# Attention and a block-quantized FFN on one core: ScalarE's jobs at the unit's end, VectorE's behind the value product

## The reference

```python
xn = layernorm(x)                                   # 4 x 1024 x 128
q, k, v = (split_heads(xn @ W + b) for W, b in ...) # 16 heads, 8 wide
scores = einsum('bhqd,bhkd->bhqk', q, k) * 8 ** -0.5 + slope[h] * (key_pos - query_pos)
attn = softmax(scores) @ v @ Wo + bo
def fp4(t):                                         # blocks of 16 along the last axis
    s = max(max(abs(t_block)) / 6, 1e-12)
    return grid[searchsorted(mid, abs(t / s))] * sign(t) * s
h = silu(fp4(xn) @ fp4(w_gate).T) * (fp4(xn) @ fp4(w_up).T)   # 352 wide
out = x + attn + fp4(h) @ fp4(w_down).T
```

## Time and profile before

| what | us |
|---|---|
| median of 3 runs | 901.35 |
| the profiled execution | 894.07 |
| its span (first to last instruction) | 892.3 |
| TensorE matmul busy | 772.9 |
| VectorE busy | 741.1 |
| ScalarE busy | 633.0 |
| GpSimd busy | 349.3 |
| mean granted TensorE clock | 0.962 |

### The profile page before, as it was taken

The page is one execution under the profiler, slowest core; times in us unless marked ns, Lnnn a source line. Parts: engine busy times, 40 slices in busy tenths (PEclk is TensorE's granted clock), DMA queues, the critical chain, the costliest instruction groups (busy, mean ns, idle before and its releaser), DMA issues.

```text
span 892.3 us, 13552 instructions
## 1 busy us (share of the span) xinstructions
PE 772.9 (87%) x4939; PEld 225.7 (25%) x4939; DVE 741.1 (83%) x878; ACT 633.0 (71%) x1262; POOL 349.3 (39%) x271
## 2 busy tenths in 40 slices
PE   3279989898989989897989989898989898979896
PEld 2012223221223323231323323222213231313222
DVE  7898898889888888978898888989897989898920
ACT  4106878777777878776877778777777687767775
POOL 7272172624226373715053553615152505141320
PEclk9557999999999999999999999999999999999999
DMA  5900020131001020320102020310102000000000
GB/s 156 256 13 2 1 72 3 52 92 36 3 13 37 13 72 2 101 44 1 37 2 49 13 73 1 107 37 1 37 2 49 13 3 1 2 1 2 2 1 24
DMA packets 32826, 31.83 MB, mean 36 GB/s; under 512 B 4344, under 2 KB 26552, under 8 KB 32760
## 3 DMA queue, kind: packets, MB, share of 16 engines
q1 hardware_dynamic: 32760, 30.96, 12.8%
HBM read 15.91 MB, written 15.04 MB: 35 GB/s over the span
## 4 chain that ended last, share of the span: by engine, by line
PE 58%; DVE 27%; ACT 8%; issue 4%; POOL 2%; DMA 1%; SPq 0%; ACTq 0%; DVEq 0%; POOLq 0%
PE low L966 22%; DVE neg_max L811 19%; PE mx L936 18%; ACT probs L630 6%; PE low L955 5%; PE mx L1005 3%; PE mx L989 3%; PE low L983 2%; DVE am L784 1%; DVE mb L804 1%; PE low L922 1%; ACT pv_s L667 1%; PE low L997 1%; DVE hid L826 1%; DVE inv L798 1%
## 5 line engine op out<-in xcount | busy, mean ns | idle before, releaser
L811 DVE TENSOR_REDUCE neg_max<-mx 128x1 f32<-128x1024 f32 x512 | 611.6, 1221 | 91.6 <-PE mx L936 80.2
L630 ACT ACTIVATE probs<-low 128x512 f32<-128x512 f32 x1024 | 552.0, 603 | 182.1 <-PE low L955 180.4
L936 PE MATMUL mx<-k_op,q_op 51*128 51x512 bf16 x1024 | 318.5, 398 | 55.9 <-DVE neg_max L811 33.4
L955 PE MATMUL low<-q_op,k_op 53*128 53x512 bf16 x1024 | 329.0, 389 | 8.0 <-ACT probs L630 2.5
L966 PE MATMUL low<-probs,v_op 128*32 128x512 f32 x2048 | 277.4, 614 | 7.1 <-ACT pv_s L667 5.9
L551 POOL TENSOR_SCALAR tanh_s<-tanh_s 128x704 f32<-128x704 f32 x16 | 31.7, 1982 | 313.7 <-ACT gate_s L681 313.7
L936 PEld LDWEIGHTS mx<-k_op,q_op 51*128 51x128 bf16 x1024 | 62.6, 95 | 358.5 <-DVE neg_max L811 197.2
L955 PEld LDWEIGHTS low<-q_op,k_op 53*128 53x128 bf16 x1024 | 68.5, 94 | 76.5 <-ACT probs L630 63.8
L489 POOL TENSOR_SCALAR mb<-mb 128x960 f32<-128x960 f32 (+2 forms) x17 | 58.8, 3456 | 39.6 <-DVE mb L804 37.9
L966 PEld LDWEIGHTS low<-probs,v_op 128*32 128x32 f32 x2048 | 40.5, 108 | 89.9 <-issue 46.1
L477 POOL TENSOR_TENSOR zb<-hid,inv 128x704 f32<-128x704 f32 x16 | 22.2, 1387 | 97.7 <-DVEq L799 97.7
(11 more groups left out here) (120 smaller groups left out, 522.3 us busy)
## 6 DMA issues: line engine op xcount, KB each, us to landing
q_op<-q_rows SPq DMA_DIRECT2D x32, 192.0 KB, 3.8
k_op<-k_rows SPq DMA_DIRECT2D x32, 192.0 KB, 4.7
q_rows<-qp SPq DMA_DIRECT2D x8, 384.0 KB, 2.6
k_rows<-kp SPq DMA_DIRECT2D x8, 384.0 KB, 3.2
x_s<-in_L_attn_inputs_dram SPq DMA_DIRECT2D x8, 256.0 KB, 3.7
q_rows<-qp SPq DMA_DIRECT2D x8, 256.0 KB, 3.1
k_rows<-kp SPq DMA_DIRECT2D x8, 256.0 KB, 3.1
out_dram<-o_s SPq DMA_DIRECT2D x8, 256.0 KB, 2.3
```

The lines of the kernel that those rows point to most:

```text
L630: nc.scalar.activation(probs[U % 3][:, 2 * g + x, :], bank("exp", U, j), ACT.Exp).then_inc(st_free, 1)
L811: nc.vector.tensor_reduce(to, slot("max", pos)[:], AX.X, ALU.max, negate=True).then_inc(mx_free, 1)
L936: ins = nc.tensor.matmul(slot("max", pos)[:, 512 * kh:512 * kh + 512], q, k, start=True, stop=True)
L955: nc.tensor.matmul(bank("exp", U, j), k_op[quad][r, g, kt * P:(kt + 1) * P], q_op[quad][r, g, half * HALF:(half + 1) * HALF], start=True, ...
```

## The change

- The unit's jobs are split in two. Jobs of ScalarE's ring (`end`) are done by TensorE behind the unit's value product and by ScalarE behind the unit's four exponentials. Jobs of VectorE's ring (`middle`) stay between the first and the second two pairs, and where a unit has one, the value product moves in front of it. In a unit without such a job the value product stays behind the last pair.
- ScalarE's copy pv_s comes behind the first exponential instead of the second.
- The lead is 23 chunks instead of 22, so one more chunk is reduced ahead of the loop and the last chunk of a half is a unit's i = 0 instead of i = 1 of the same unit. `HEAD` follows from the lead's parity, so that a chunk and the score beside it still use opposite row halves. The turn jobs stay in the same units.
- In a period up moves one unit later (5 instead of 4), the block maxima behind the second chunk of that unit, scales and inverses to unit 6, powers to unit 8, and GpSimd's steps with them. The projections start at unit 9 of a period instead of 3: xnT, q, k at 9, 10, 11 and v at 3 of the next; the splits of q and k follow both behind each other. SyncE's issues of parts and gathers hang on `group_unit` and move six units later.
- The inverses become a function of their own (`block_inverses`), behind the second chunk.

```diff
-LEAD = 22
+LEAD = 23
...
 def group_unit(g):
-    return 13 + 60 * (g // 2 - 1) + 15 * (g % 2)
+    return 19 + 60 * (g // 2 - 1) + 15 * (g % 2)
...
-HEAD = ((1, 0), (1, 1), (0, 0), (0, 1))
+HEAD = tuple((x, g) for x in ((LEAD + 1) % 2, LEAD % 2) for g in range(2))
...
     if 0 <= p < NP:
-        out += {0: [("xT", p)], 1: [("gate", p, 0)], 2: [("gate", p, 1)], 4: [("up", p)], 12: [("hT", p, 0)],
+        out += {0: [("xT", p)], 1: [("gate", p, 0)], 2: [("gate", p, 1)], 5: [("up", p)], 12: [("hT", p, 0)],
                 13: [("hT", p, 1)], 14: [("down", p)]}.get(f, [])
     for g in range(2, NG):
-        if 0 <= U - group_unit(g) < 4:
-            out.append((("xnT", "q", "k", "v")[U - group_unit(g)], g))
+        out += {0: [("xnT", g)], 1: [("q", g)], 2: [("k", g)], 9: [("v", g)]}.get(U - group_unit(g), [])
...
+def middle(U):
+
+    return [job for job in extras(U) if job[0] in IN_DVE_RING]
+
+
+def end(U):
+
+    return [job for job in extras(U) if job[0] not in IN_DVE_RING]
...
(rings)
-            for job in extras(U) if i == 0 else ():
-                (to_dve if job[0] in IN_DVE_RING else to_act)(*job)
+            for job in middle(U) if i == 0 else ():
+                to_dve(*job)
+        for job in end(U):
+            to_act(*job)
...
(GpSimd)
-                    if U == group_unit(g) + 2:
+                    if U == group_unit(g) + 4:
                         three_parts(g, 0, "q")
-                    if U == group_unit(g) + 3:
+                    if U == group_unit(g) + 4:
                         three_parts(g, 1, "k")
...
-                    if U == ffn_unit(p) + 5:
+                    if U == ffn_unit(p) + 6:
                         scale_to_grid(p + 1)
-                    if U == ffn_unit(p) + 7:
+                    if U == ffn_unit(p) + 8:
                         round_on_grid(p + 1)
...
(ScalarE)
-                for j in range(2):
+                for j in range(4):
                     exponential(U, j)
-                if U % KT == 1 and U > KT:
-                    m = U // KT - 1
-                    act.wait_ge(pv_done, U - 1)
-                    if m:
-                        act.wait_ge(mx_full, MX["pvT", m - 1] + 1)
-                    nc.scalar.copy(pv_s[:], pv).then_inc(pv_kept, 1)
-                for job in extras(U):
+                    if j == 0 and U % KT == 1 and U > KT:
+                        m = U // KT - 1
+                        act.wait_ge(pv_done, U - 1)
+                        if m:
+                            act.wait_ge(mx_full, MX["pvT", m - 1] + 1)
+                        nc.scalar.copy(pv_s[:], pv).then_inc(pv_kept, 1)
+                for job in end(U):
...
-                for j in range(2, 4):
-                    exponential(U, j)
...
(VectorE)
-                link(nc.vector.reciprocal(inv[:, 0:n], scn[:, 0:n]))
-                dve.sem_inc(inv_ok, 1)
+
+            def block_inverses(job):
+                n = job_cols(job) // BLK
+                settle()
+                nc.vector.reciprocal(inv[:, 0:n], scn[:, 0:n]).then_inc(inv_ok, 1)
...
-                    if i == 1:
-                        for job in extras(U):
-                            job_on_vector(job)
+                    for job in middle(U) if i == 1 else ():
+                        job_on_vector(job)
                     if pos < CHUNKS:
                         reduce_chunk(pos)
                     for p in range(NP):
-                        if U == ffn_unit(p) + 5 and i == 0:
+                        if U == ffn_unit(p) + 5 and i == 1:
                             block_maxima(p + 1)
-                        if U == ffn_unit(p) + 5 and i == 1:
-                            block_scales(p + 1)
-                        if U == ffn_unit(p) + 7 and i == 0:
+                        if U == ffn_unit(p) + 6:
+                            (block_scales if i == 0 else block_inverses)(p + 1)
+                        if U == ffn_unit(p) + 8 and i == 0:
                             powers(p + 1)
...
(TensorE)
-                    for job in extras(U) if i == 0 else ():
+                    if 0 < U <= NU and i == (0 if middle(U) else 1):
+                        value_product(U - 1)
+                    for job in middle(U) if i == 0 else ():
                         job_on_array(job)
-                if 0 < U <= NU:
-                    value_product(U - 1)
+                for job in end(U):
+                    job_on_array(job)
```

More of the change, by code:

```diff
@@ L795, in block_scales @@
                 mark(nc.vector.tensor_scalar(sc[:, 0:n], am[:, 0:n], 1.0 / 6.0, 1e-12, ALU.mult, ALU.max))
-                link(nc.vector.tensor_scalar(scn[:, 0:n], am[:, 0:n], (1.0 + 2.0 ** -22) / 6.0, 1e-12,
+                mark(nc.vector.tensor_scalar(scn[:, 0:n], am[:, 0:n], (1.0 + 2.0 ** -22) / 6.0, 1e-12,
                                              ALU.mult, ALU.max))
-                link(nc.vector.reciprocal(inv[:, 0:n], scn[:, 0:n]))
-                dve.sem_inc(inv_ok, 1)
+            def block_inverses(job):
+                n = job_cols(job) // BLK
+                settle()
+                nc.vector.reciprocal(inv[:, 0:n], scn[:, 0:n]).then_inc(inv_ok, 1)
             def powers(job):
@@ L872, in _ @@
             block_scales(0)
+            block_inverses(0)
             for pos in range(LEAD):
```

## The result

| | before | after |
|---|---|---|
| median of the runs, us | 900.57 (898.9 to 916.8, 4 runs) | 922.95 (919.77 to 924.45, 4 runs) |
| the profiled execution, us | 894.07 | 919.77 |
| its span | 892.3 | 918.0 |
| main loop, first score of unit 0 to first score of unit 255 | 66.67 to 880.36: 813.7 | 68.08 to 906.07: 838.0 |
| VectorE busy | 741.1 | 723.5 |

The ratio is 1.0255, 95% interval 1.0222 to 1.0288: slower by 22.4 us in the medians. The ratio leaves out executions that lie more than 1.5% above the fastest of their kernel, such as the one of 916.8 us. Of the 25.7 us between the two spans, 24.3 are in the main loop and 1.4 ahead of it, where one more chunk is reduced.

What follows compares the result with a forecast made beforehand. A loop of score, exponential, score, value product was taken to set 2.46 us per unit without a job. Terms summed to +20 us on 894.1 profiled, so 914; the runs' median lies 7.3 higher, so 921, range 898 to 942.

Steps and rivals of the forecast that it cites:

- gates at the end: 32 gate products behind the value product: each costs 1.08 us instead of 0.49, +18.9 us in all.
- projections at the end: xnT, q, k, v of six groups at the unit's end and in other units: +3.0 a group, +18 us.
- turn: 31 turn transposes at the unit's end: -7.4 us for place, -5 for TensorE's wait for neg_parts going, -12.4 together.
- product ahead of pvT, wo, bvo: Value product ahead of pvT fills TensorE's hole: -0.32 us for two units, some 20 times, -6.4 us.
- product ahead of up: In 16 units up's data come 1.0 us later; VectorE's holes leave 0.3 of it: +5 us.
- product ahead of down: In 16 units with down, 0.4 us each, estimated from up: +6.4 us.
- pv_s copy: ScalarE's copy behind the first exponential: value product 0.49 us earlier, except in 10 of 31 halves: -10.3 us.
- stretches at half clock: Shorter TensorE waits avoid an estimated three stretches at 1.2 GHz, 1 us each: -3 us.
- hT: 32 jobs of three transposes, about 0.5 us each at the unit's end, cost what a job costs now: 0.
- The first (slack covers the end jobs): Rival: VectorE or other slack covers gates and projections at the unit's end: 884 us on the runs' scale; chance 0.11.
- the second: Rival: maxima reach the scores late, each half waits 1 us: +31, 952 us; chance 0.07.
- the third: Rival: ten more stretches at half clock, 1.5 us each: +15, 936 us; chance 0.1.

Runs made afterwards that it cites:

- experiment 1: Kernel after with only the gate products back in the middle of their units: 906.32 us, ratio 1.0064.
- 2: Kernel after with xnT, q, k and v back in the middle, at the kernel after's units: 910.09 us, ratio 1.0105.
- 10: Kernel after with only the turn jobs back in the middle, lead 23 kept: 926.13 us, ratio 1.0275.
- 3: Kernel after with the value product last in every unit: 909.96 us, ratio 1.0099.
- experiment 9: Kernel after with the value product last again only in units with up: 906.86 us, ratio 1.0073.
- 5: Kernel after with the pv_s copy back behind the second exponential: 934.29 us, ratio 1.0383.
- experiment 11: Kernel before with only the pv_s copy moved behind the first exponential: 905.44 us, ratio 1.0084.
- 7: Kernel after with lead 22 instead of 23: 920.94 us, ratio 1.0236.
- 4: Kernel after with all of ScalarE's jobs in the middle, value product first only where all jobs are VectorE's: 918.66 us, ratio 1.0199.
- 6: Kernel after with only the hT transposes back in the middle: 934.15 us, ratio 1.0414.
- the mixture: Kernel after with gates, xnT, q, k, v, ctxT in the middle, value product first only for pvT, wo, bvo: 877.02 us, ratio 0.9785.

## Why the prediction was right, and where it was not

The time, the sign and the range came out (921 predicted, 922.95 measured), and most unit lengths that it named are in the trace: gates 3.25 and 3.57, pvT 2.87 and 2.71, pv_s 2.62, k 3.7 to 3.9, VectorE idle 1.2 ahead of `hid`. That the time came within 2 us is in part luck: the sum gave 914 us for the profiled execution, which took 919.77, and the 7.3 us that were added for the median of the runs are 3.2 in the kernel after. Term by term up was taken 9 us too low and turn's saving too high, and gates and projections were taken a little too high. The measured columns are what undoing a part in the kernel after gave, once by the medians against before and once by the unit lengths in the traces with the units at half clock left out:

| term | predicted | by the medians | by the units | run |
|---|---|---|---|---|
| gates at the end | +18.9 | +16.6 | +16.2 | 1 |
| projections at the end | +18 with the move | +12.9, the place alone | +10.0, and about +5 for the move | 2 |
| turn | -12.4 | -6.1, the place alone | -3.4 to -5, the place alone | 10 |
| product ahead of pvT, wo, bvo | -6.4 | -6.8 | -7.2 | 3 and 9 |
| product ahead of up | +5 | +13.2 | +13.8 | 9 |
| product ahead of down | +6.4 | | +6.6 | 3 |
| pv_s copy | -10.3 | -9.4 | -11.1 | 5 |
| stretches at half clock | -3 | | about -4 | before and after |
| one more chunk ahead of the loop | +1.2 | | +1.4 | span |

By the units the terms sum to +24 to +26 without the last line; the loops differ by 24.3. The medians differ by 22.4. The column by the medians has an error of some us in each line. Each part was undone with all others in place, so a sum need not be exact, and experiment 11 shows how far a term can depend on its surroundings.

- **Gates.** Right in mechanism and size: +0.30 and +0.62 in the two units, the rest in the successor. The 2 to 3 us that are missing are not worked out; some of the units behind a pair are paced by VectorE anyway.
- **Projections.** Right: 4.4 - 1.4 = 3.0 a group was predicted, and 4.2 - 1.4 = 2.8 is what the one group that can be compared shows. The runs undo the place only, 1.7 to 2.2 a group; the rest is the move.
- **Turn.** The place was taken at 7.4 us and gives some 5. The step "lead 23 puts the last chunk of a half at the start of a unit ..., so TensorE's wait of 19.4 us for neg_parts goes" came true in the wait, but experiments 7 and 10 show that the wait stays away without lead 23 and all but stays away without the end place. What took it away, and what its going is worth (the prediction counted 5), is open: no run brings it back.
- **Up.** The step that failed is "the rest of the 1.0 that was lost is what those holes don't take: I take 0.3". Of the 1.0 between 0.6 and 1.0 is lost in twelve periods, and the whole term is 13.8 us instead of 5; near its upper bound of 16. The 5% of idle time in VectorE's stretch is hardly a hole behind up: the unit behind up is the very one in which TensorE waits for VectorE. And "in four units the product waits for pv_s in front of a job: +1" was too low: it is 1.0 in each of the four, 4.0 us, half of it at up and half at down.
- **Product ahead of pvT.** Right to 0.02 us in the pair of units that was worked out, and in the sum to about 1 us, the output projections included.
- **pv_s.** The size was right for the kernel after. The step is silent on the condition: it holds because no job of ScalarE's ring is in the middle any more. In the kernel before the same edit gives nothing.
- **hT.** "They cost what a job costs now" held, but hides a dependence: the powers' later place would have cost some 15 us if hT had stayed in the middle (17.7 and 17.6 us in its units in experiments 4 and 6). The +2 for GpSimd's rounding, whose end was to come within a few tenths of the first hT, did not come: hT waits 0.4 us in all.
- **Clock.** The stretches at half clock in the loop went from four to one, as "-3" supposed: the units with such a stretch give 3.9 us back between the two traces. That shorter waits of TensorE are the reason is not shown, and the other variants of the kernel after have one to eight. In experiment 9 one such stretch makes the unit in which it lies 1.3 us longer and the one that is gone 1.0 shorter.
- **The rivals.** The first (slack covers the end jobs) is refuted by experiment 1; the second by the waits, where no score waits for the maxima's DMAs; the third by the clock.
- **The range.** Its upper end does not follow from what it names: 936 with up and down at their upper bounds is 953, not 942. The result did not test it.

Open: what the projections' move does beyond the one group read above, what up's move to unit 5 does by itself, what took the wait for `neg_parts` away, and whether the mixture gains more if the copy stands behind the second exponential in just the units with a job in the middle, as experiment 11 suggests; none of them was tried.

## What to carry to other kernels

Price a job by the hole it stands in: in a loop of score, exponential, score, value product a job in the middle costs one exponential (0.49 us) because it runs while TensorE would wait for ScalarE, and at the end it costs its whole time plus the delay of the next exponential. What is put into a hole delays the engine that the job feeds; if the unit behind waits for that engine, most or all of the delay comes out (0.6 to 1.0 of 1.0 us here), however much idle time an average over a stretch shows. And one edit can be worth something only after another, or a wait can stay away whichever of two edits is undone, so undo parts one at a time, undo both where neither alone brings the wait back, and try one alone in the kernel before.

## What the runs showed of the hardware

Every trace here is at half clock from 25 to 28 us on for 48 to 55 us, which takes in the first units of the loop. Inside the loop a stretch at half clock is mostly 3.4 us long, and it costs 0.2 to 1.2 us where the units are otherwise the same (experiments 1, 2 and 9). In experiment 11 one lasted 23.9 us (856.5 to 880.4), though TensorE was busy for 9.94 and 10.00 of 10 us in it. It began behind a stretch in which TensorE had been busy for 1.63 of 3 us (853 to 856); in the kernel before the same units followed 2.63 busy of 4 us, and the clock stayed at 1.00. Why the clock fell and stayed low is not shown. At 1.2 GHz the six units took 9.6 us more. The Trainium skill, "TensorE: Matmul & The Clock Gate", Part 1, says in its trace caveats that the clock gate has been seen stuck for 50 us and more, at a quarter, and that the trace's events of it can be unreliable. This trace has a long stretch at a half, and there the units really are longer. One profiled execution shows it; that nine of this kernel's ten executions have a mean granted clock of 0.945 to 0.955 (nine of 19 of the kernel before have 0.930 to 0.956) suggests that such losses are not rare, but not in what form they come.
